# Inverting the 16-row diagonal blocks on VectorE, one block on a partition, with a round trip through DRAM

## The reference

```python
def step(carry, kvq):
    W, b = carry
    k, v, q = kvq
    pred = W @ k + b
    g = 2.0 / d_h * (pred - v)
    W = W - LR * jnp.outer(g, k)
    b = b - LR * g
    out = W @ q + b
    return ((W, b), out)
...
h = jax.nn.gelu(jnp.einsum('bsd,edf->ebsf', x, W1) + b1[:, None, None, :], approximate=False)
y_e = jnp.einsum('ebsf,efd->ebsd', h, W2) + b2[:, None, None, :]
y = jnp.einsum('ebsd,bse->bsd', y_e, P_norm)
```

## Time and profile before

| what | us |
|---|---|
| three runs | 500.49, 502.99, 502.44 (median 502.44) |
| the profiled execution: its own time | 503.49 |
| its span in the trace | 501.5 |
| PE busy | 459.9 (92%) |
| PEld busy | 391.8 (78%) |
| DVE busy | 293.6 (59%) |
| ACT busy | 216.2 (43%) |
| POOL busy | 163.2 (33%) |

### The profile page before, as it was taken

How to read it: one execution, slowest core, us unless ns; L and a number is a source line. 1 busy time by engine, 2 the same in 40 slices (tenths; PEclk the granted TensorE clock), 3 DMA queues, 4 the chain that set the end, 5 groups by cost and what they waited for, 6 DMA issues and landing times. The chain is left out here.

```text
span 501.5 us, 10488 instructions
## 1 busy us (share of the span) xinstructions
PE 459.9 (92%) x3296; PEld 391.8 (78%) x3296; DVE 293.6 (59%) x1076; ACT 216.2 (43%) x529; POOL 163.2 (33%) x234
## 2 busy tenths in 40 slices
PE   6898989999999999999997987899999999999874
PEld 5696868887978988889876886788888888888721
DVE  6788888875776848667787853123333333232317
ACT  3364355455463545433434221344444444444402
POOL 8700033015033140340514341034344444444420
PEclk8999999999899999999999999999999999999987
DMA  6799100001000010000000042012221222222466
GB/s 187 239 284 166 30 23 22 1 12 33 1 23 23 7 38 0 23 23 2 33 12 29 17 118 53 13 55 53 61 68 53 66 62 65 65 58 64 142 218 211
DMA packets 37172, 33.23 MB, mean 66 GB/s; under 512 B 5380, under 2 KB 29832, under 8 KB 37128
## 3 DMA queue, kind: packets, MB, share of 16 engines
q1 hardware_dynamic: 32432, 23.66, 18.6%
q0 software_dynamic: 4352, 8.99, 5.3%
q10 hardware_dynamic: 344, 0.03, 0.1%
HBM read 17.32 MB, written 15.34 MB: 65 GB/s over the span
## 5 line engine op out<-in xcount | busy, mean ns | idle before, releaser
L615 POOL DMA_INDIRECT routed<-send,slot x64 | 63.4, 991 | 147.6 <-DVE send L1339 69.3
L624 POOL DMA_INDIRECT results<-nat,y_to x72 | 70.0, 972 | 109.0 <-DVE nat L1490 95.2
L937 PE MATMUL psA<-xuT,w_all 128*128 128x256 f32 x288 | 72.3, 393 | 10.5 <-issue 6.5
L950 PE MATMUL psB<-w_all,h1T 128*128 128x128 f32 x576 | 70.4, 275 | 1.0 <-ACT h1T L1130 1.0
L937 PEld LDWEIGHTS psA<-xuT,w_all 128*128 128x128 f32 x288 | 51.3, 189 | 23.6 <-ACT h1T L1130 13.1
L1130 ACT ACTIVATE h1T<-psA,b1T 128x256 f32<-128x256 f32 x144 | 57.2, 474 | 26.7 <-PE psB L950 17.6
L950 PEld LDWEIGHTS psB<-w_all,h1T 128*128 128x128 f32 x576 | 67.1, 192 | 1.2 <-ACT h1T L1130 1.1
L1462 DVE TENSOR_SCALAR xu<-ring 128x256 f32 (+1 forms) x38 | 11.2, 296 | 75.9 <-DMA ring<-routed 63.8
L1121 ACT ACTIVATE xuT<-psB 128x256 f32<-128x256 f32 x37 | 14.2, 384 | 60.7 <-PE psB L927 53.6
L762 PE MATMUL psB<-xnT,w_l 128*128 128x512 f32 x64 | 33.9, 611 | 0.5 <-ACT selT L1049 0.5
L774 PE MATMUL psB<-w_l,hg0T 128*128 128x128 f32 x256 | 33.0, 282 | 0.0
(11 more groups left out here) (274 smaller groups left out, 941.2 us busy)
## 6 DMA issues: line engine op xcount, KB each, us to landing
ring<-routed SPq DMA_DIRECT2D x38, 130.0 KB
w_all<-results SPq DMA_DIRECT2D x15, 256.0 KB, 4.2
routed<-ring SPq DMA_DIRECT2D x24, 130.0 KB, 6.6
w_all<-in_L_ffn_W_dram SPq DMA_DIRECT2D x1, 2048.0 KB, 10.4
out_dram<-x_all SPq DMA_DIRECT2D x8, 256.0 KB, 2.3
results<-nat,y_to POOLq DMA_INDIRECT x72
...
routed<-send,slot POOLq DMA_INDIRECT x64
```

Of the source, the lines that this page charges most:

```text
L615: pool.indirect_dma_start(routed[:, :], bass.IndirectOffsetOnAxis(ap=slot[par][:, c, t:t + 1], axis=0), send[par][:, c, t, :], None).then_ ...
L624: pool.indirect_dma_start(results[:, :], bass.IndirectOffsetOnAxis(ap=y_to[:, par, a:a + 1], axis=0), yw[:, par, a, :], None).then_inc(S[f ...
L937: last = mm(psA[:, j // 2, (j % 2) * UNIT:(j % 2 + 1) * UNIT], w1_all[:, e, j * P:(j + 1) * P], xuT[:, :], start=True, stop=True)
L950: last = mm(psB[:, 1, col(a)], h1T[:, k, a * P:(a + 1) * P], w2_all[:, f * JF + k, :], start=(k == 0), stop=(k == JF - 1))
```

## The change

VectorE inverts the 16 x 16 diagonal blocks, 32 of them in a group (4 tiles x 8 blocks), one on a partition. For that SP stores N of the group to DRAM (`n_room`), loads its diagonal blocks to 32 partitions (`n_base`), stores the inverses and their transposes into the diagonal blocks of a zeroed room (`inv_room`), and loads both whole matrices of the group (`inv`, which holds `xinvT` and `xinv`). This is `base_blocks(g)` on SP and step `base` on DVE. PE starts at level 4 (`FIRST`), after a wait on `inv_in`. Levels 0 to 3, step `one`, and their parts on PE, ACT, DVE and POOL are gone. One room serves all groups, so SP handles one group at a time. Psum psC, freed of the levels, takes the output of the units; there, `out` goes over k outside and over the halves inside, and counts `h1_free` up after each k. The 4.5 MB of weights are issued within `base_blocks` of groups 1, 2 and 3, behind `n_base`. POOL waits for the filling of `routed` by itself. `ORDER` is another table.

```diff
--- before.py
+++ after.py
...
+BASE = 16
+FIRST = BASE.bit_length() - 1
+BLOCKS = P // BASE
+DIAG = BASE * (BASE + 1)
+TILE_ROOM = BLOCKS * BASE * (P + 1)
 NEWTON = 3
-JOINS_C = 3
...
-    "6 half4", "7 kT", "7 qT", "7 slots", "6 join4", "7 gram_n", "7 gram_q", "6 half5", "7 gram_x", "6 join5",
...
+    "7 landed", "7 copies", "9 tok", "7 gram_n", "6 join4", "7 slots", "6 half5", "7 qT", "6 join5", "7 base",
+    "7 gram_q", "6 turn", "7 send 0", "6 half6", "7 gram_x", "6 join6", "6 u1", "6 cross", "7 send 1", "6 u2",
+    "6 out", "7 half4", "7 join4", "7 send 2", "7 half5", "7 send 3", "U first", "7 join5", "U hid 0",
...
+    n_room = nc.dram_tensor("n_room", (TILES, TILE_ROOM), F32, kind="Internal").ap()
+    inv_room = nc.dram_tensor("inv_room", (2, TILES, TILE_ROOM), F32, kind="Internal").ap()
+
+    def whole_rows(room):
+        return room[..., 0:P * P]
+
+    def diagonal_blocks(room):
+
+        return (room.rearrange("t (b x) -> (t b) x", b=BLOCKS)[:, 0:BASE * P]
+                .rearrange("n (r c) -> n r c", c=P)[:, :, 0:BASE])
...
-            sp.dma_start(w1_all[:, :, :], W1.rearrange("e d f -> d e f")).then_inc(w_l1, 16)
-            sp.dma_start(w2_all[:, :, :], W2.rearrange("e f d -> (e f) d")
-                         .rearrange("(k p) d -> p k d", p=P)).then_inc(w_l1, 16)
-            sp.dma_start(b2_all[:, :, :].rearrange("p e d -> p (e d)"),
-                         b2.rearrange("(a e) d -> a (e d)", a=1).broadcast_to([P, E * D])).then_inc(w_l1, 16)
-
             sp.wait_ge(consts, 3)
+            sp.dma_start(whole_rows(inv_room).rearrange("k t (p c) -> p (k t) c", p=P),
+                         ring[:, :, :, 0:D].rearrange("p r a d -> p (r a) d")).then_inc(inv_zeroed, 16)
             for e in range(E):
                 for n in range(MIN_UNITS):
                     at = e * REGION + n * UNIT
                     sp.dma_start(routed[at:at + UNIT, :].rearrange("(a p) d -> p a d", p=P),
                                  ring[:, n + 1 if n else e % 2, :, :]).then_inc(prefilled, 16)
-            sp.wait_ge(prefilled, 16 * E * MIN_UNITS)
-            sp.sem_inc(ring_given, 1)
+
+            def base_blocks(g):
+
+                par = g % 2
+                wait_on(sp, "n_ready", g + 1)
+                sp.dma_start(whole_rows(n_room).rearrange("t (p c) -> p t c", p=P), nT[par][:, :, :]).then_inc(n_out, 16)
+                sp.wait_ge(n_out, 16 * (g + 1))
+                sp.dma_start(n_base[:, 0:BASE * BASE].rearrange("n (r c) -> n r c", c=BASE),
+                             diagonal_blocks(n_room)).then_inc(n_base_in, 16)
+                if g == 1:
+                    sp.dma_start(w1_all[:, :, :], W1.rearrange("e d f -> d e f")).then_inc(w_l1, 16)
+                elif g == 2:
+                    sp.dma_start(w2_all[:, :, :], W2.rearrange("e f d -> (e f) d")
+                                 .rearrange("(k p) d -> p k d", p=P)).then_inc(w_l1, 16)
+                elif g == 3:
+                    sp.dma_start(b2_all[:, :, :].rearrange("p e d -> p (e d)"),
+                                 b2.rearrange("(a e) d -> a (e d)", a=1).broadcast_to([P, E * D])).then_inc(w_l1, 16)
+                if g == 0:
+                    sp.wait_ge(inv_zeroed, 16)
+                else:
+                    sp.wait_ge(inv_in, 16 * g)
+                sp.sem_inc(apart, 1)
+                wait_on(sp, "base_ready", g + 1)
+                for k in range(2):
+                    sp.dma_start(diagonal_blocks(inv_room[k]),
+                                 inv_base[:, k, 0:BASE * BASE].rearrange("n (r c) -> n r c", c=BASE)
+                                 ).then_inc(inv_out, 16)
+                sp.wait_ge(inv_out, 32 * (g + 1))
+                if g >= 2:
+                    sp.sem_inc(apart, 1)
+                    wait_on(sp, "u2_ps", g - 1)
+                sp.dma_start(inv[par].rearrange("p k t c -> p (k t) c"),
+                             whole_rows(inv_room).rearrange("k t (p c) -> p (k t) c", p=P)).then_inc(inv_in, 16)
+
+            for g in range(groups):
...
+                base_blocks(g)
...
-                if step == "one":
-
-                    ready("kT_ps")
-                    pool.tensor_copy(xinvT[par][:, :, :], ident[:, :].unsqueeze(1).broadcast_to([P, TILES, P])
-                                     ).then_inc(S["one_ready"], 1)
...
                 elif step.startswith("half"):
                     lv = int(step[4:])
-                    ps = (psC if lv <= JOINS_C else psD)[:, 0, :]
-                    if lv == 1:
-                        ready("cross_ready")
-                    if lv == JOINS_C + 1 and g == 0:
-                        wait_on(pe, "res_ready", FIRST_X)
-                        wait_on(pe, "lg1_read", FIRST_X)
-                    ready(f"xinv{lv - 1}_ready")
+                    if lv == FIRST:
+                        if g == 0:
+                            wait_on(pe, "res_ready", FIRST_X)
+                            wait_on(pe, "lg1_read", FIRST_X)
+                        pe.wait_ge(inv_in, 16 * (g + 1))
+                    else:
+                        ready(f"xinv{lv - 1}_ready")
...
                 elif step.startswith("join"):
                     lv = int(step[4:])
-                    c = 0 if lv <= JOINS_C else 1
-                    if lv == 1:
-                        ready("qk_ready")
-                    if lv == JOINS_C + 1 and g:
+                    if lv > FIRST:
+                        ready(f"xinvT{lv - 1}_ready")
+                    elif g:
                         wait_on(pe, "s1_ready", g)
-                    ready(f"xinvT{lv - 1}_ready")
                     ready(f"p{lv}_ready")
...
             def out(u, f, e):
 
                 wait_on(pe, "yb_ready", u)
-                for a in range(HALVES):
-                    for k in range(JF):
-                        if a == 0:
-                            wait_on(pe, "gelu_ready", u * JF + k + 1)
-                        last = mm(psB[:, 1, col(a)], h1T[:, k, a * P:(a + 1) * P],
+                for k in range(JF):
+                    wait_on(pe, "gelu_ready", u * JF + k + 1)
+                    for a in range(HALVES):
+                        last = mm(psC[:, a, 0:D], h1T[:, k, a * P:(a + 1) * P],
                                   w2_all[:, f * JF + k, :], start=(k == 0), stop=(k == JF - 1))
-                        if a:
-                            last.then_inc(S["h1_free"], 1)
+                    last.then_inc(S["h1_free"], 1)
...
+                n, u, u_t = n_base[:, :], inv_base[:, 0, :], inv_base[:, 1, :]
+                link(v.tensor_copy(within(u, 2, 0, 1, 1, 1)[:, :, 0, :], within(n, 2, 0, 1, 1, 1)[:, :, 0, :]))
+                for size in (1 << lv for lv in range(2, FIRST)):
+                    h, count = size // 2, BASE // size
+                    for row in reversed(range(h)):
+                        k = size - 1 - row
+                        terms = base_terms[:, 0:count * h * k].rearrange("n (i c j) -> n i c j", c=h, j=k)
+                        link(v.tensor_tensor(
+                            terms, within(n, size, row, row + 1, 1, k).broadcast_to([TILES * BLOCKS, count, h, k]),
+                            within(u, size, row + 1, h, k, h).rearrange("n i j c -> n i c j"), ALU.mult))
+                        link(v.tensor_reduce(within(u, size, row, h, 1, h)[:, :, 0, :], terms, AX.X, ALU.add))
+                h = BASE // 2
+                cube = [TILES * BLOCKS, h, h, h]
+                terms = base_terms[:, :].rearrange("n (r c j) -> n r c j", r=h, c=h)
+                high, low, corner = (within(u, BASE, 0, 0, h, h)[:, 0], within(u, BASE, h, h, h, h)[:, 0],
+                                     within(u, BASE, 0, h, h, h)[:, 0])
+                link(v.tensor_tensor(terms, within(n, BASE, 0, h, h, h)[:, 0].unsqueeze(2).broadcast_to(cube),
+                                     low.rearrange("n j c -> n c j").unsqueeze(1).broadcast_to(cube), ALU.mult))
+                link(v.tensor_reduce(base_half[:, :, :], terms, AX.X, ALU.add))
+                link(v.tensor_tensor(terms, high.unsqueeze(2).broadcast_to(cube),
+                                     base_half[:, :, :].rearrange("n j c -> n c j").unsqueeze(1).broadcast_to(cube),
+                                     ALU.mult))
+                link(v.tensor_reduce(corner, terms, AX.X, ALU.add))
+                whole = BASE * BASE
+                v.tensor_copy(u_t[:, 0:whole].rearrange("n (r c) -> n r c", c=BASE),
+                              u[:, 0:whole].rearrange("n (c r) -> n r c", r=BASE)).then_inc(S["base_ready"], 1)
...
-                    wait_apart(g + 1, "one_ready", "n_ready")
-                    v.copy_predicated(blocks(xinvT[par], 0, 1), odd_mask(0),
-                                      blocks(nT[par], 0, 1)).then_inc(S["xinvT0_ready"], 1)
-                    ready("xinvT0_ready")
-                    v.transpose(xinv[par][:, :, :], xinvT[par][:, :, :]).then_inc(S["xinv0_ready"], 1)
```

(6 more changed lines are left out.)

87 lines of the change are left out of this document (54 added, 33 removed), and 89 rows, old and new, of the table ORDER.

## The result

The changed kernel takes 475.45 us, median of 4 runs (473.17 to 476.49); the kernel before, on the same chip, 502.03 (4 runs). Ratio 0.9467, 95% interval 0.9425 to 0.951. Forecast: 476. The profiled execution took 475.52 us, with a span of 473.8; the profile of before had a span of 501.5.

What follows compares the result with a forecast made beforehand. PE was taken to bound both stages, with DVE close behind in the first. 503.5 - 27 (first stage) + 12.4 (seam) - 12 (units) = 476.9 for the profiled execution, so 476; range 470 to 488, with neighbouring rivals 455 to 498.

Steps and rivals of the forecast that it cites:

- PE's 44 us: Levels 1 to 3 on PE: 48 steps removed, priced by distances of starts, 24 x 1.00 + 24 x 0.84 us.
- the first stage (-27): 60 us to group 7's N: busier of PE and DVE at 90%, 203 us in place of 230; ends 15 and 41.
- DVE's +9 (41 gone, 50 come): DVE over eight groups: 41 us of mask copies and transposes gone, `base` new at 6.3 us a group, 50 in all.
- third rival: DVE in the first stage: `base` costs 9.5 us through slow strided, transposed reads, DVE bounds; 501 us; chance 0.12.
- The trip: N's round trip through DRAM, per group: last load issued 14.8 us after N, level 4 at 19, covered in groups 0 to 6.
- fourth rival: Uncovered round trip, PE waiting at "half4" of each group; 6 us covered, slower from x = 8.6 us extra; chance 0.08.
- The seam (+12.4): Group 7's N to first unit: SP's fillings and bounds queue behind its last load, 33.6 us in place of 21.2.
- The units (-12): 36 units after the seam: earlier gelus let `hid` start without waiting; 12 us gained over 30 units, ends 0 and 16.
- the 0.40 a unit: Gain taken per unit, where PE's weight loads stood still 0.45 us before `hid` and a unit took 4.29.
- The floor of 3.6 us by the ring: Units: the ring's loop of loads, `xu`, `y_wt` and two DVE operations as new lower limit per unit.
- The rival of 97% (460 us): First stage: PE and DVE interlock at 97%, gaining 41 us there, 14 in the units, 12.4 back; chance 0.22.
- The rule on weight loads: Pricing PE's removed steps by the skill page's rule: weight loads give 47 us, plain matmul busy time 52.

Runs made afterwards that it cites:

- e1: Changed kernel with the old order of loops in the units' `out` (halves outside, k inside), writes still in psC: 487.22 us, ratio 0.9689.
- e10: Changed kernel with 16 idle products of `ident` on PE ahead of group 7's level 4 and 30 ahead of the first unit: 473.64 us, ratio 0.9418.
- e11: Changed kernel with SP's eight fillings of `routed` split around group 7's trip, plus 16 idle products on PE ahead of its level 4: 469.95 us, ratio 0.9329.
- e6: Changed kernel with 24 products of `ident` a group added on PE, some 45 us in all: 509.46 us, ratio 1.0121.
- e4: Changed kernel without the arithmetic of `base`, identities sent through the round trip instead: 463.04 us, ratio 0.9199.
- e7: Changed kernel with each `base` computed twice on DVE, same result: 541.09 us, ratio 1.0749.
- e5: Changed kernel with N stored to DRAM twice, one store after the other, in each group's round trip: 478.55 us, ratio 0.9541.
- e2: Kernel before with only the units' new loop order and output in psC, end sums taking banks in another order: 488.79 us, ratio 0.9718.

## Why the prediction was right

**PE's 44 us and the first stage (-27).** The gain was 21.7 us in the profiled execution (N 269.4 for 291.1), and 25.5 to 26.4 where the clock held (e1, e10, e11), against a forecast N of 264. The term was mis-sized by 5 us, and some 4 of these are PE's lower clock, which nothing in the text had. The mechanism was right: e6 confirms that PE's work was what counted, and e4 that taking work from DVE gains little.

That N came within 2 us of the forecast where the clock held is in part luck, as two inputs were off and cancelled. PE's work from 60 us to N was taken as 183 us and was 189.0 in e10 (192.9 in the changed kernel, at the lower clock), since PE did 4 us less before 60, where the prediction counted nothing. And PE was busy 92% of that stretch, not 90%.

Of the 44 us, 38.5 lie ahead of group 7's N (seven groups of eight). PE's busy time from the start to N was 275.4 us before and 236.1 to 238.0 where the clock held (e1, e10, e11): 37.4 to 39.3 less. Of the 350 records fewer there, 336 are the levels' (seven groups, six steps of eight records), so little other work crossed N, and the 44 is borne out, though not measured by itself.

**DVE's +9 (41 gone, 50 come).** `base` was 6.8 us, not 6.3: the 0.5 is the two products at 1.02 and 1.07 instead of 0.71 each, less some 0.2 elsewhere. The third rival had named transposed reads; they were slow, but by 0.3 to 0.4 us each, 0.7 a group and not 3.2. e7 shows how near it was: each further us on DVE ahead of N cost a whole one and more.

**The trip.** Forecast 14.8 us to the last load's issue, measured 283.62 - 269.38 = 14.2; 19 to level 4, measured 18.7. That level 4 came as forecast is half a coincidence, as PE ended group 6's work at the same time. The load of `inv`, taken at 4.2 between 2.3 and 10.4, took 4.2; the stores, bounded by 2.7, took 2.2. In the groups it was covered nearly whole: from 60 to 269 PE waited for `inv` twice, 1.0 and 0.9 us. The fourth rival thus fell; e5, with 2.3 us more, did not reach it either, which fits its 6 us of cover. The Trainium skill ("DMA: Bandwidth & Descriptors", "Specifications") says that below 512 bytes the engine reads, modifies and writes. Here 32 KB in runs of 64 bytes landed in 2.2 us, 256 KB in plain rows in 2.3; no store of 32 KB in long runs is there to compare, so what the short runs cost by themselves, in latency or in rate, no run shows.

**The seam (+12.4).** The first unit's distance from N grew by 11.1 us (32.21 for 21.16). SP's part was forecast at 15.4 from the last load to the ring's; measured 298.96 - 283.62 = 15.3. The sum treated this as lost one for one. The two pairs of kernels that differ in the seam and not in the loop bracket that: by N to end, e1 lies 220.8 - 210.4 = 10.4 us over the kernel before, and the changed kernel 204.4 - 196.5 = 7.9 over e2. The same steps of group 7 stand ahead of the first unit and behind it in all four, so no work was moved out of the way; the 7.9 is lower because e2's 29 units took 110.8 us for 109.2 and its end 1.2 more.

**The units (-12).** From the first unit to the end 17.0 us were gained, 15.6 of them in the 29 units behind the 8th transpose; the loop's own part is 13.8 by e2 and 16.5 by e1. The mechanism was right: the waits of the weight loads for ACT are gone, and come back with the old order (e1). The size was not. The term that was off is the 0.40 a unit, which measured 4.29 - 3.73 = 0.56 in the steady stretch: the prediction took the 0.45 us for which the weight loads stood still as the whole cost, and in e1 such a stop lengthens the unit by 0.53. The floor of 3.6 us by the ring did not bind. The 17.0 lies 1 us over the term's upper end of 16.

**Sum.** -21.75 + 11.05 - 17.0 = -27.7, the difference of the spans, 501.5 - 473.8. Forecast: -26.6. Part of the closeness is luck: the first stage gave 5 less and the units 5 more than forecast, and the seam cost 1.4 less.

The rival of 97% (460 us) failed: PE was busy 92%, and even e4, with no `base` arithmetic at all, reached 463.

**The rule on weight loads.** The prediction turned the section "Identifying the Most-Contended Engine" of the Trainium skill's page "Perfetto Trace Analysis" into a price for a removed step. The page says something narrower: which share of a window tells how close an engine is to its limit, and that pipelined matmuls look smaller in the trace. Here the plain sum of their busy times, 52 us, is larger than their distances of starts, 44. Seven eighths of 44, 47 (weight loads) and 52 are 38.5, 41 and 45.5, and PE's busy time ahead of N fell by 37.4 to 39.3: that sides with the distances of starts, as far as little else crossed N.
